# Sorted experts of a routed MLP: tokens stationary and gate and up moved together as 256 columns, the loop written out, deeper rings, 47 tiles

## The chip, the core and the metric

The program runs on one core of a Trainium2 chip. The metric is the device time of one execution in microseconds (us); a lower number is better. Nothing runs on the other cores.

## The reference, cut to what matters

The program computes two layers over 2048 tokens of width 512: a state-space layer with a routed MLP behind it, then attention with a quantised MLP behind it, each followed by a layer norm. The change lies in the routed MLP alone:

```python
gate = zeros((T, E)).at[arange(T)[:, None], idx].add(vals)      # the best 2 of 16 experts per token
def step(y, p):
    w1, b1, w2, b2, w3, b3, ge = p
    h = silu(xt @ w1 + b1) * (xt @ w2 + b2)                     # 512 -> 128, twice
    return y + ge[:, None] * (h @ w3 + b3), None                # 128 -> 512
y, _ = scan(step, zeros_like(xt), (ew1, eb1, ew2, eb2, ew3, eb3, gate.T))
```

## The kernel before, in words

`program` calls the stages one after the other, each in a block of its own that all engines leave together: `ssm`, `normalise` (ln1), `route_and_share`, `sorted_experts`, `normalise` (ln2, which gathers the experts' rows), `project`, `attend`, `attention_out`, `normalise` (ln3), `quantised_mlp`. In `route_and_share` each token's row is scattered twice into `sorted_x` in HBM, sorted by expert and padded so that every run of 128 rows (a tile, `P`) belongs to one expert; `g.owner` holds the expert of each tile. `SORTED` (L30) is the number of tiles, 47 rounded up to a multiple of `TURN`, so 48.

`sorted_experts` (L1199) works through these tiles. Per tile j it loads 256 KB of rows and 769 KB of weights and biases of the owner (gate and up: the first `WUP` = 1024 columns; down: the next 512), computes, and stores 256 KB. Every product is made in three matmuls of float32r parts (`three`, L126): stationary and moving operand are each split into a high part (a rounded copy) and a low part (the rest), and high·high, high·low and low·high are summed in PSUM.

The steps of tile j, with the function that issues each:

- SP: `load_x`, `load_w`, `store_y`. `load_w` waits until the buffer of tile j-4 is free (`up_lo`, `down_lo`, `h_ready`), reads the owner into a register and issues the DMA. Four weight buffers and four row buffers. In SP's order `store_y` comes 4 tiles late, behind the two loads of the same step.
- PE: `turn` (four 128x128 transposes of the rows), `up` (gate and then up, 4 chunks by 3 matmuls each: the weights are stationary, the turned tokens move as 128 columns, 24 matmuls in all; gate and up come out with the hidden unit in the partition), `down` (3 matmuls of 512 columns, the hidden activations stationary).
- ACT: `x_hi` (L1344), `down_weights_hi` (L1350), `gate` (silu, L1356), `h_hi` (L1363), `y_copy` (L1338).
- DVE: `x_lo` (L1376), `up_weights_lo` (L1381), `hidden` (L1387), `h_lo` (L1392).
- POOL: `up_weights_hi` (L1281), `down_weights_lo` (L1287).

`steps` sets the order on each engine: a list of (lag, function) pairs, so that step n does tile n - lag of each. The first `TURN` steps and the last are written out; those between run in a hardware loop (`Fori`) with four tiles in the body and semaphore values computed from the loop's register. Before: SP (0, load_x) (0, load_w) (4, store_y); PE (0, turn) (1, up) (2, down); ACT (3, y_copy) (0, x_hi) (1, down_weights_hi) (1, gate) (1, h_hi); DVE (0, x_lo) (0, up_weights_lo) (1, hidden) (1, h_lo); POOL (0, up_weights_hi) (1, down_weights_lo). The split weights `g.wh`, `g.wl` have two buffers, and so have the turned tokens, the hidden parts, `y` and each PSUM tile. `SORTED` also sets how many zero tiles `ssm` stores into `sorted_x` and the width of the small owner computation in `route_and_share`.

Of the kernel before, what the change touches and what calls it, by code (L numbers as in the profile page):

```python
# [8 lines left out]
F32 = mybir.dt.float32  # L9
# [5 lines left out]
P = 128  # L15
# [13 lines left out]
TURN = 4  # L29
SORTED = -(-(TOP * TILES + EXPERTS - 1) // TURN) * TURN  # L30
# [640 lines left out]
def normalise(nc, g, tag, by_feature, out=None, quantise=False, gather=False, ahead=None):  # L671
# [5 lines left out]
    with ExitStack() as ctx:  # L677
# [215 lines left out]
def route_and_share(nc, a, g):  # L893


    with ExitStack() as ctx:
# [49 lines left out]
        turned, gate_ready, dve_chain, scattered = sem("turned"), sem("gate_ready"), sem("dve_chain"), sem("scattered")  # L946
# [252 lines left out]
def sorted_experts(nc, a, g):  # L1199
# [4 lines left out]
    with ExitStack() as ctx:  # L1204
        sb, ps, sem = scoped(nc, ctx, "exp", reused=True)
        raw = g.raw + [sb(f"raw{k}", [P, WN + 2]) for k in range(2, TURN)]
        x = [sb(f"x{k}", [P, DIM]) for k in range(TURN)]
# [4 lines left out]
        y = [sb(f"y{k}", [P, DIM]) for k in range(2)]  # L1212
        pt = [ps(f"pt{k}", [P, KC, P]) for k in range(2)]

        pgu = [[ps(f"p{n}{k}", [P, NB]) for n in "gu"] for k in range(2)]
        py = [ps(f"py{k}", [P, DIM]) for k in range(2)]
        x_in, w_in = [sem(f"x_in{k}") for k in range(TURN)], [sem(f"w_in{k}") for k in range(TURN)]
        up_hi, down_hi, xh_ready, g_ready = sem("up_hi"), sem("down_hi"), sem("xh_ready"), sem("g_ready")
        s_ready, hh_ready, hl_ready = sem("s_ready"), sem("hh_ready"), sem("hl_ready")


        y_stored = [sem(f"y_stored{k}") for k in range(2)]
        x_turned, xl_ready, u_ready, h_ready = sem("x_turned"), sem("xl_ready"), sem("u_ready"), sem("h_ready")
        up_lo, down_lo, y_ready, y_copied = sem("up_lo"), sem("down_lo"), sem("y_ready"), sem("y_copied")
        AHEAD = TURN
        block = ctx.enter_context(nc.Block())

        def steps(eng, stages):

            for n in range(TURN):  # L1230
                for lag, do in stages:
                    if n >= lag:
                        do(n - lag, n - lag)
            with eng.Fori(1, SORTED // TURN) as i:
                for n in range(TURN):
                    for lag, do in stages:
                        do(i * TURN + (n - lag), (n - lag) % TURN)
            for n in range(max(lag for lag, _ in stages)):
                for lag, do in stages:
                    if n < lag:  # L1240
                        do(SORTED + n - lag, (n - lag) % TURN)

        @block.sync
        def _(sp):
            def load_x(j, s):

                sp.wait_ge(x_turned, j - TURN + 1 + AHEAD)
                sp.dma_start(x[s][:].unsqueeze(1), g.sorted_x.rearrange("(t p) d -> p t d", p=P)[:, bass.ds(j, 1), :]
                             ).then_inc(x_in[s], 16)

            def load_w(j, s):

                sp.wait_ge(up_lo, j - TURN + 1 + AHEAD)
                sp.wait_ge(down_lo, j - TURN + 1 + AHEAD)
                sp.wait_ge(h_ready, j - TURN + 1 + AHEAD)
                e = nc.values_load(g.owner[0:1, bass.ds(j, 1)], engines=(mybir.EngineType.SP,), min_val=0,
                                   max_val=EXPERTS - 1)
                sp.dma_start(raw[s][:].unsqueeze(1), a["w123"][bass.ds(e, 1)].rearrange("e p w -> p e w")
                             ).then_inc(w_in[s], 16)

            def store_y(j, s):
                sp.wait_ge(y_copied, j + 1 + AHEAD)
                sp.dma_start(g.sorted_y.rearrange("(t p) d -> p t d", p=P)[:, bass.ds(j, 1), :], y[s % 2][:].unsqueeze(1)
                             ).then_inc(y_stored[s % 2], 16)

            for k in range(2):
                sp.sem_inc(y_stored[k], 16)
            steps(sp, [(0, load_x), (0, load_w), (TURN, store_y)])
            for k in range(2):
                sp.wait_ge(y_stored[k], 16 * SORTED // 2 + 16)  # L1270

        @block.gpsimd
        def _(pool):
            pool.sem_inc(down_lo, AHEAD)

            def up_weights_hi(j, s):

                pool.wait_ge(w_in[s], (j - s) * (16 // TURN) + 16)

                wait_apart(pool, u_ready, j - 1 + AHEAD)  # L1280
                nc.gpsimd.tensor_scalar(g.wh[s % 2][:, 0:WUP], raw[s][:, 0:WUP], 1.0, 0.0, ALU.mult,  # L1281
                                        ALU.add).then_inc(up_hi, 1)

            def down_weights_lo(j, s):
                pool.wait_ge(down_hi, j + 1)
                wait_apart(pool, y_ready, j - 1 + AHEAD)
                nc.gpsimd.tensor_tensor(g.wl[s % 2][:, WUP:WN], raw[s][:, WUP:WN], g.wh[s % 2][:, WUP:WN].bitcast(F32),  # L1287
                                        ALU.subtract).then_inc(down_lo, 1)
# [983 lines left out]
```

## Time and profile before

| | us |
|---|---|
| runs | 2175.79, 2177.35, 2159.76 |
| median | 2175.79 |
| profiled execution | 2182.81 (span 2181.1) |
| mean granted TensorE clock | 0.908 of full |
| busy: PE / DVE / ACT / POOL | 83% / 72% / 38% / 36% of the span |

The stage of this change runs from its first DMA issue at 659.7 to the next stage's first instructions at 901.8 us of the span. A line of a timeline gives start, duration, engine, line of the kernel, operation and tiles (out<-in); matmuls overlap, so the distance between two starts is what one costs. The 1.2 and 2.4 GHz levels of TensorE's clock are shown as 0.50 and 1.00.

### The profile page before, as it was taken

The page shows a single profiled execution, that of the slowest core. Times are in us where ns is not written, and L with a number is a line of the kernel's source. Part 1 is how long each engine was busy: PE and PEld are TensorE (multiplying, and loading weights), DVE is VectorE, ACT ScalarE, POOL GpSimd, SP SyncE. Part 2 cuts the span into 40 slices and gives each one's busy share as a digit, 9 for nine tenths or more (in the row PEclk, how much of TensorE's full clock was granted, in tenths as well). Part 3 has the DMA queues.
Part 4 walks back from the last instruction along what each step waited for, and adds up shares of the span by engine and source line. Part 5 has one row for each costly group of instructions (what it writes and reads, how often), then busy time and mean ns, then how long its engine had stood idle before and what let it go on. Part 6 is the DMA issues. An engine that isn't in the chain of part 4 may idle for free. (4 is left out here: it accounts for less than half of the span.)

```text
span 2181.1 us, 26434 instructions
## 1 busy us (share of the span) xinstructions
PE 1810.3 (83%) x8264; PEld 1133.3 (52%) x8264; DVE 1567.4 (72%) x2851; ACT 832.6 (38%) x1362; POOL 779.1 (36%) x469
## 2 busy tenths in 40 slices
PE   5888878776598999539958888888936999999998
PEld 1232323224367888428833333333724877777786
DVE  6999999996435765582138888887388677667668
ACT  4646464432113544312217777777232111111112
POOL 4898989862504766551011000000033133212200
PEclk7999989998787987759969999999966999999999
DMA  4333334220306887535553333331001000000002
GB/s 126 103 116 97 116 107 115 83 62 19 137 17 225 300 287 257 187 120 194 193 158 96 88 97 85 93 92 46 1 31 44 15 30 30 30 1 30 1 1 78
DMA packets 111213, 212.99 MB, mean 98 GB/s; under 512 B 18953, under 2 KB 35721, under 8 KB 110203
## 3 DMA queue, kind: packets, MB, share of 16 engines
q1 hardware_dynamic: 105979, 194.80, 28.6%
q0 software_dynamic: 5120, 16.78, 2.4%
q8 instruction: 58, 0.95, 0.2%
q14 instruction: 56, 0.46, 0.1%
HBM read 145.92 MB, written 63.18 MB: 96 GB/s over the span
## 5 line engine op out<-in xcount | busy, mean ns | idle before, releaser
L1773 DVE TENSOR_REDUCE att_top<-att_first 128x1 f32<-128x512 f32 x512 | 332.3, 686 | 101.9 <-PE att_first L1653 94.3
L552 DVE TENSOR_TENSOR_SCAN ssm_h<-ssm_da,ssm_dbx 128x512 f32<-128x512 f32 x256 | 305.5, 1212 | 6.4 <-ACT ssm_da L422 6.1
L292 POOL TENSOR_TENSOR ssm_dbx<-ssm_u,ssm_bbc 128x2048 f32<-128x2048 f32 x63 | 285.0, 4524 | 47.9 <-DVE ssm_h L552 46.4
L635 PE MATMUL ssm_y<-ssm_hc,all_ident 128*128 128x512 f32 x396 | 228.7, 667 | 73.9 <-DVE ssm_hc L503 68.9
L1735 ACT ACTIVATE att_prob<-att_second 128x1024 f32<-128x1024 f32 x256 | 248.0, 1022 | 86.6 <-PE att_second L1673 81.2
L422 ACT ACTIVATE ssm_da<-ssm_dt,ssm_minus_a 128x512 f32<-128x512 f32 x256 | 176.7, 690 | 200.8 <-DVE ssm_h L552 200.5
L1919 POOL TENSOR_TENSOR pairs_raw<-pairs_raw,pairs_scales 128x512 f32<-128x512 f32 x42 | 42.2, 1040 | 532.1 <-DMA pairs_raw<-in_w 532.1
L2049 ACT ACTIVATE ffn_silu<-ffn_pg 128x256 f32<-128x256 f32 x112 | 43.1, 385 | 415.4 <-PE ffn_pg L130 415.3
L1653 PE MATMUL att_first<-att_ks,att_qs 48*128 48x512 f32 x512 | 133.6, 510 | 63.2 <-DVE att_top L1773 48.4
L128 PE MATMUL ffn_pg<-pairs_wh,last_XH 128*128 128x512 f32 x448 | 180.1, 402 | 1.7 <-PEq L677 1.7
L129 PE MATMUL ffn_pg<-pairs_wl,last_XH 128*128 128x512 f32 x448 | 178.8, 399 | 0.0
L130 PE MATMUL ffn_pg<-pairs_wh,last_XL 128*128 128x512 f32 x448 | 178.1, 397 | 0.0
L635 PEld LDWEIGHTS ssm_y<-ssm_hc,all_ident 128*128 128x128 f32 x396 | 65.8, 201 | 186.7 <-DVE ssm_hc L503 131.6
L1653 PEld LDWEIGHTS att_first<-att_ks,att_qs 48*128 48x128 f32 x512 | 53.5, 190 | 192.2 <-DVE att_top L1773 131.4
L2073 DVE TENSOR_TENSOR ffn_h<-ffn_pg,ffn_silu 128x256 f32<-128x256 f32 x112 | 47.4, 423 | 134.6 <-ACT ffn_silu L2049 134.5
L503 DVE TENSOR_TENSOR ssm_hc<-ssm_cbc,ssm_h 128x512 f32<-128x512 f32 x198 | 132.5, 669 | 14.2 <-issue 7.1
L1688 PE MATMUL att_out<-att_prob,att_v 128*32 128x512 f32 x1024 | 137.2, 608 | 0.1
L1926 POOL TENSOR_SCALAR pairs_wh<-pairs_raw 128x512 fp32r<-128x512 f32 x42 | 24.9, 625 | 238.7 <-PE ffn_py L130 238.7
L128 PE MATMUL ffn_py<-pairs_wh,ffn_hh 128*128 128x512 f32 x224 | 97.8, 437 | 0.2 <-DVE ffn_hl L2091 0.2
L130 PEld LDWEIGHTS ffn_pg<-pairs_wh,last_XL 128*128 128x128 f32 x448 | 85.5, 191 | 21.7
L128 PEld LDWEIGHTS ffn_pg<-pairs_wh,last_XH 128*128 128x128 f32 x448 | 85.0, 190 | 22.4 <-issue 2.0
L129 PEld LDWEIGHTS ffn_pg<-pairs_wl,last_XH 128*128 128x128 f32 x448 | 85.0, 190 | 20.7
(294 smaller groups left out, 4095.5 us busy)
## 6 DMA issues: line engine op xcount, KB each, us to landing
mlps_raw<-in_w SPq DMA_DIRECT2D x26, 769.0 KB, 5.8
exp_raw<-in_w SPq DMA_DIRECT2D x24, 769.0 KB, 5.8
ssm_bbc<-brow_dram SPq DMA_DIRECT2D x64, 256.0 KB, 4.1
ssm_cbs<-crow_dram SPq DMA_DIRECT2D x58, 256.0 KB, 3.5
sorted_x<-ssm_zero SPq DMA_DIRECT2D x48, 256.0 KB, 3.7
exp_x<-sorted_x SPq DMA_DIRECT2D x48, 256.0 KB, 3.8
sorted_y<-exp_y SPq DMA_DIRECT2D x48, 256.0 KB, 3.3
att_qs<-qk_dram SPq DMA_DIRECT2D x192, 64.0 KB, 2.2
```

Of the source, the lines that this page charges most:

```text
L128: pe.matmul(out, lh, rh, start=first, stop=False)
L129: pe.matmul(out, lh, rl, start=False, stop=False)
L130: return pe.matmul(out, ll, rh, start=False, stop=last)
L292: nc.gpsimd.tensor_tensor(dbx[:, n % 2], u[:, n // STATE % 2], bbc[:, n % RING, :].unsqueeze(1).to_broadcast([P, KC, NB]), ALU.mult).then_ ...
L422: nc.scalar.activation(da[:, i % 2, :], dt[:, b % 2, c, :], ACT.Exp, scale=minus_a[:, c, n % STATE:n % STATE + 1]).then_inc(da_ready, 1)
L503: nc.vector.tensor_tensor(hc[:, k % 2, :], cbc[:], h[:, n % 2, c, :], ALU.mult).then_inc(hc_ready, 1)
L552: nc.vector.tensor_tensor_scan(h[:, n % 2, c, :], da[:, i % 2, :], dbx[:, n % 2, c, :], 0.0, ALU.mult, ALU.add).then_inc(h_ready, 1)
L635: pe.matmul(y[:, c, :], g.ident[:], hc[:, k % 2, :], start=(m == 0), stop=(m == STATE - 1)).then_inc(y_own, 1)
L1653: pe.matmul(p_first[first_place(m) % FIRSTS][:], qs[w % RING][at, pair, qt * P:(qt + 1) * P], ks[w % RING][at, pair, :], start=True, stop= ...
L1688: mm = pe.matmul(p_out[VPAD * j:VPAD * (j + 1), :], v[s % RING][:, kt, VPAD * j:VPAD * (j + 1)], prob[step % 2][:, j, :], start=(kt == 0), ...
L1735: nc.scalar.activation(prob[step % 2][:, js, :], p_second[second_place(step, pair) % 2][:], ACT.Exp, scale=DK ** -0.5).then_inc(exp_done, 1)
L1773: nc.vector.tensor_reduce(top[w % 2][:, qt, item:item + 1], p_first[first_place(m) % FIRSTS][:], AX.X, ALU.max).then_inc(max_done, 1)
```

## The change

The gate and up product is turned round: the turned tokens are stationary, and the gate and up weights of one 128-row chunk move together as 256 columns, so `up` has 12 matmuls of 256 columns. The result has the token in the partition; it is copied from PSUM to SBUF by ACT (`copy_gu`), turned back by two transposes on PE (`turn_gu`), and read from PSUM by `gate` and `hidden`. The hardware loop is replaced by steps that are all written out, with constant semaphore values. Weight buffers: 7, five of them inside `g.X`; row buffers 6; y buffers 4; split down weights 4, two of them inside `g.XL`. The store is issued 8 steps late. 47 tiles. Some DMA semaphores are made once for the whole program.

```diff
-TURN = 4
-SORTED = -(-(TOP * TILES + EXPERTS - 1) // TURN) * TURN
+SORTED = TOP * TILES + EXPERTS - 1
...
-            gathered = [sem(f"gathered{k}") for k in range(GRING)]
+            gathered = g.gathered
...
+        RAWS, XS, DOWNS, YS = 7, 6, 4, 4
+        GU = 2 * INTER
...
+        raw = ([r[:] for r in g.raw] + [inside(g.X[:], k) for k in range(5)])
+        x = [sb(f"x{k}", [P, DIM]) for k in range(XS)]
+        gu = [sb(f"gu{k}", [P, GU]) for k in range(2)]
+        y = [sb(f"y{k}", [P, DIM]) for k in range(YS)]
+        spare = g.XL[:].rearrange("p c t -> p (c t)")
+        down_h = [g.wh[k][:, WUP:WN] for k in range(2)] + [spare[:, k * DIM:(k + 1) * DIM] for k in range(2)]
+        down_l = [g.wl[k][:, WUP:WN] for k in range(2)] + [spare[:, k * DIM:(k + 1) * DIM] for k in range(2, 4)]
+        pgu = [ps(f"pgu{k}", [P, NB]) for k in range(2)]
+        pr = [ps(f"pr{k}", [P, NB]) for k in range(2)]
...
+        def steps(stages):
+            for n in range(SORTED + max(lag for lag, _ in stages)):
+                for lag, do in stages:
+                    if 0 <= n - lag < SORTED:
+                        do(n - lag)
...
+            def load_w(j):
+                if j >= RAWS:
+                    sp.wait_ge(up_lo, j - RAWS + 1)
+                    sp.wait_ge(down_lo, j - RAWS + 1)
+                    sp.wait_ge(h_ready, j - RAWS + 1)
...
-            steps(sp, [(0, load_x), (0, load_w), (TURN, store_y)])
+            steps([(0, load_x), (0, load_w), (RAWS + 1, store_y)])
...
+            def up_weights_hi(j):
+                arrived(pool, w_in, j)
+                if j >= 2:
+                    pool.wait_ge(gu_ready, j - 1)
...
             def down_weights_lo(j):
                 pool.wait_ge(down_hi, j + 1)
-                wait_apart(pool, y_ready, j - 1 + AHEAD)
...
-                for n, ready in ((0, g_ready), (1, u_ready)):
-                    for c in range(KC):
-                        w = slice((n * KC + c) * INTER, (n * KC + c + 1) * INTER)
-                        mm = three(pe, pgu[k][n][:, 0:P], g.wh[k][:, w], g.wl[k][:, w], xh[k][:, c, :], xl[k][:, c, :],
-                                   c == 0, c == KC - 1)
-                    mm.then_inc(ready, 1)
+                if j >= 2:
+                    pe.wait_ge(gu_copied, j - 1)
+                both = [w[k][:, 0:WUP].rearrange("p (n c i) -> p c n i", n=2, c=KC) for w in (g.wh, g.wl)]
+                out = pgu[k][:, 0:GU].rearrange("p (n i) -> p n i", n=2)
+                for c in range(KC):
+                    mm = three(pe, out, xh[k][:, c, :], xl[k][:, c, :], both[0][:, c], both[1][:, c], c == 0, c == KC - 1)
+                mm.then_inc(gu_ready, 1)
+
+            def turn_gu(j):
+                pe.wait_ge(gu_copied, j + 1)
+                if j >= 2:
+                    pe.wait_ge(h_ready, j - 1)
+                for n in range(2):
+                    mm = pe.transpose(pr[j % 2][:, n * P:(n + 1) * P], gu[j % 2][:, n * P:(n + 1) * P], g.ident[:])
+                mm.then_inc(gu_turned, 1)
...
-            steps(pe, [(0, turn), (1, up), (2, down)])
+            steps([(0, turn), (2, turn_gu), (1, up), (3, down)])
...
+            def copy_gu(j):
+                act.wait_ge(gu_ready, j + 1)
+                if j >= 2:
+                    act.wait_ge(gu_turned, j - 1)
+                nc.scalar.activation(gu[j % 2][:], pgu[j % 2][:, 0:GU], ACT.Copy).then_inc(gu_copied, 1)
+
+            def y_copy(j):
+                act.wait_ge(y_ready, j + 1)
+                if j >= YS:
+                    act.wait_ge(y_stored[j % YS], 16 * (j // YS))
+                nc.scalar.activation(y[j % YS][:], py[j % 2][:], ACT.Copy).then_inc(y_copied, 1)
...
-            steps(act, [(3, y_copy), (0, x_hi), (1, down_weights_hi), (1, gate), (1, h_hi)])
+            steps([(0, x_hi), (2, gate), (0, down_weights_hi), (2, h_hi), (1, copy_gu), (3, y_copy)])
...
-            steps(dve, [(0, x_lo), (0, up_weights_lo), (1, hidden), (1, h_lo)])
+            steps([(0, x_lo), (2, hidden), (0, up_weights_lo), (2, h_lo)])
...
+        g.scattered, g.gathered = sem("scattered"), [sem(f"gathered{k}") for k in range(4)]
```

POOL's list is as before, (0, up_weights_hi) (1, down_weights_lo).

## Rows read from the trace of the kernel before

**Rows 1.** Windows: busy us and instruction count of each engine, granted clock, DMA share, GB/s.
```profile
659.70:901.80 242.10, 217.10 (x1488) 202.90 (x1488) 145.87 (x192) 106.90 (x240) 147.03 (x96) 0.86 0.78 260
721.00:775.00 54.00, 48.13 (x381) 44.70 (x381) 39.47 (x50) 25.87 (x61) 37.30 (x25) 1.00 0.91 312
857.80:877.80 20.00, 20.00 (x87) 18.81 (x87) 8.90 (x13) 7.17 (x16) 10.01 (x6) 0.50 0.63 207
664.00:673.00 9.00, 5.55 (x25) 5.18 (x26) 4.61 (x4) 1.48 (x3) 3.33 (x3) 0.50 0.98 378
773.00:776.00 3.00, 1.41 (x12) 1.24 (x10) 2.62 (x3) 0.95 (x3) 1.38 (x2) 0.95 0.89 321
722.00:725.00 3.00, 1.68 (x16) 1.56 (x15) 1.88 (x3) 1.25 (x3) 1.25 (x2) 1.00 0.92 336
```

**Rows 2.** Weight tiles, whole stage: POOL's rounding; duration min/median/max, first and last start.
```profile
L1281 POOL TENSOR_SCALAR mlps_wh<-mlps_raw x24: 1038/1046/1122, 666.2 to 880.2; 128x1024 fp32r<-128x1024 f32 x24
L1281 POOL TENSOR_SCALAR mlps_wh<-exp_raw x24: 1039/1047/1097, 674.1 to 889.3; 128x1024 fp32r<-128x1024 f32 x24
```

**Rows 3.** Timeline of PE at full clock, 783.8 to 785.4.
```profile
783.76 0.27 PE L130 MATMUL exp_pu<-exp_xh,mlps_wl 128*128 128x128 f32 x1
...
784.43 0.28 PE L130 MATMUL exp_pu<-exp_xh,mlps_wl 128*128 128x128 f32 x1
...
785.07 0.40 PE L130 MATMUL exp_py<-mlps_wh,exp_hl 128*128 128x512 f32 x1
785.31 0.60 PE L1303 MATMUL exp_pt<-all_ident,exp_x 128*128 128x128 f32 x4
```

**Rows 4.** Timeline of PE at half clock, 781.4 to 781.7.
```profile
781.47 0.41 PE L129 MATMUL exp_pg<-exp_xl,mlps_wh 128*128 128x128 f32 x1
781.68 0.41 PE L130 MATMUL exp_pg<-exp_xh,mlps_wl 128*128 128x128 f32 x1
```

**Rows 5.** DMA, 721 to 775: queue share, then issues, KB each, median us to landing.
```profile
q1 hardware_dynamic: 5570, 16.84, 91.3%
...
mlps_raw<-in_w SPq DMA_DIRECT2D x7, 769.0 KB, 5.9
exp_raw<-in_w SPq DMA_DIRECT2D x6, 769.0 KB, 5.6
```

**Rows 6.** Waits, 721 to 775, and SP's own wait, 700 to 880: total us, times, longest.
```profile
POOL mlps_wh L1281 <- DMA mlps_raw<-in_w: 5.3, 4, 2.0
...
SPq L1263 <- ACT exp_y L1338: 79.2, 38, 4.8
```

**Rows 7.** Groups of ACT by form, 721 to 775: busy us, mean ns | idle before.
```profile
L1344 ACT ACTIVATE exp_xh<-exp_pt 128x512 fp32r<-128x512 f32 x12 | 7.1, 591 | 0.0
L1338 ACT ACTIVATE exp_y<-exp_py 128x512 f32<-128x512 f32 x12 | 7.0, 587 | 0.9 <-issue 0.5 <-PE exp_py L130 0.4
L1363 ACT ACTIVATE exp_hh<-exp_h 128x128 fp32r<-128x128 f32 x13 | 4.0, 311 | 28.2 <-DVE exp_h L1387 28.2
L1350 ACT ACTIVATE mlps_wh<-exp_raw 128x512 fp32r<-128x512 f32 x6 | 3.8, 632 | 0.0
L1356 ACT ACTIVATE exp_silu<-exp_pg,exp_raw 128x128 f32<-128x128 f32 x6 | 2.2, 368 | 0.0
```

**Rows 8.** From the page's costliest groups: an ACT read of 256 PSUM columns, in another stage.
```profile
L2049 ACT ACTIVATE ffn_silu<-ffn_pg 128x256 f32<-128x256 f32 x112 | 43.1, 385 | 415.4 <-PE ffn_pg L130 415.3
```

**Rows 9.** Groups of DVE by form, 721 to 775.
```profile
L1376 DVE TENSOR_TENSOR exp_xl<-exp_pt,exp_xh 128x512 fp32r<-128x512 f32 x12 | 8.3, 692 | 6.0 <-ACT exp_xh L1344 6.0
L1392 DVE TENSOR_TENSOR exp_hl<-exp_h,exp_hh 128x128 fp32r<-128x128 f32 x12 | 7.2, 596 | 4.5 <-ACT exp_hh L1363 4.5
L1387 DVE SCALAR_TENSOR_TENSOR exp_h<-exp_pu,exp_raw,exp_silu 128x128 f32<-128x128 f32 x7 | 2.4, 344 | 0.0
```

**Rows 10.** Splitting of weights, whole stage: duration ns min/median/max.
```profile
L1381 DVE TENSOR_TENSOR mlps_wl<-exp_raw,mlps_wh x24: 1215/1216/2315, 676.1 to 890.4; 128x1024 fp32r<-128x1024 f32 x24
L1287 POOL TENSOR_TENSOR mlps_wl<-exp_raw,mlps_wh x24: 1267/2254/2346, 683.4 to 894.5; 128x512 fp32r<-128x512 f32 x24
```

More of the change, by code:

```diff
@@ L1218, in sorted_experts @@
[L1218 to L1225, printed above, removed]
+        x_in, w_in = [sem(f"x_in{k}") for k in range(XS)], [sem(f"w_in{k}") for k in range(RAWS)]
@@ L1226, in sorted_experts, with arrived @@
         block = ctx.enter_context(nc.Block())
-        def steps(eng, stages):
-            for n in range(TURN):
+        def arrived(eng, sems, j):
+            eng.wait_ge(sems[j % len(sems)], 16 * (j // len(sems) + 1))
+        def steps(stages):
+            for n in range(SORTED + max(lag for lag, _ in stages)):
                 for lag, do in stages:
[L1232 to L1241, printed above, removed]
+                    if 0 <= n - lag < SORTED:
+                        do(n - lag)
@@ L1243, in _ @@
         @block.sync
         def _(sp):
[L1245 to L1259, printed above, removed]
@@ L1359, in h_hi, with x_hi @@
-            def h_hi(j, s):
-                act.wait_ge(h_ready, j + 1 + AHEAD)
-                act.wait_ge(y_ready, j - 1 + AHEAD)
-                nc.scalar.activation(hh[s % 2][:], h[s % 2][:], ACT.Copy).then_inc(hh_ready, 1)
-            steps(act, [(3, y_copy), (0, x_hi), (1, down_weights_hi), (1, gate), (1, h_hi)])
+            def x_hi(j):
+                act.wait_ge(x_turned, j + 1)
+                if j >= 2:
+                    act.wait_ge(gu_ready, j - 1)
+                nc.scalar.activation(xh[j % 2][:], pt[j % 2][:], ACT.Copy).then_inc(xh_ready, 1)
@@ new lines, in gate, with down_weights_hi @@
+            def gate(j):
+                act.wait_ge(gu_turned, j + 1)
+                if j >= 2:
+                    act.wait_ge(h_ready, j - 1)
+                nc.scalar.activation(silu[j % 2][:], pr[j % 2][:, 0:INTER], ACT.Silu,
+                                     bias=raw[j % RAWS][:, WN:WN + 1]).then_inc(s_ready, 1)
+            def down_weights_hi(j):
+                arrived(act, w_in, j)
+                if j >= DOWNS:
+                    act.wait_ge(y_ready, j - DOWNS + 1)
+                nc.scalar.activation(down_h[j % DOWNS], raw[j % RAWS][:, WUP:WN], ACT.Copy).then_inc(down_hi, 1)
@@ new lines, in h_hi @@
+            def h_hi(j):
+                act.wait_ge(h_ready, j + 1)
+                if j >= 2:
+                    act.wait_ge(y_ready, j - 1)
+                nc.scalar.activation(hh[j % 2][:], h[j % 2][:], ACT.Copy).then_inc(hh_ready, 1)
+            def copy_gu(j):
+                act.wait_ge(gu_ready, j + 1)
+                if j >= 2:
+                    act.wait_ge(gu_turned, j - 1)
+                nc.scalar.activation(gu[j % 2][:], pgu[j % 2][:, 0:GU], ACT.Copy).then_inc(gu_copied, 1)
@@ L1373, in x_lo, with hidden @@
-            def x_lo(j, s):
+            def x_lo(j):
                 dve.wait_ge(xh_ready, j + 1)
-                nc.vector.tensor_tensor(xl[s % 2][:], pt[s % 2][:], xh[s % 2][:].bitcast(F32),
+                nc.vector.tensor_tensor(xl[j % 2][:], pt[j % 2][:], xh[j % 2][:].bitcast(F32),
                                         ALU.subtract).then_inc(xl_ready, 1)
-            def up_weights_lo(j, s):
+            def hidden(j):
+                dve.wait_ge(s_ready, j + 1)
+                if j >= 2:
+                    dve.wait_ge(hl_ready, j - 1)
+                nc.vector.scalar_tensor_tensor(out=h[j % 2][:], in0=pr[j % 2][:, INTER:GU], scalar=raw[j % RAWS][:, WN + 1:WN + 2],
+                                               in1=silu[j % 2][:], op0=ALU.add, op1=ALU.mult).then_inc(h_ready, 1)
```

113 lines of the change are left out of this document (44 added, 69 removed).

## Prediction

> **What bounds the kernel now.** I read the windows over the stage first, then PE's timeline, the DMA queues, the waits, and the groups of ACT, DVE and POOL. In the windows [rows 1] the stage of the sorted experts takes 242.1 us of the 2181 us span; PE is busy for 90% of it, at a mean clock of 0.86, and the DMA share is 0.78. That mean hides two regimes. From 721 to 775 the clock is full and the DMA queues are at 0.91 and 312 GB/s; from 857.8 to 877.8 the clock is half, PE never stops, and DMA falls to 0.63. The pace follows from POOL's first instruction on each tile, which starts at 666.2 for tile 0 and at 889.3 for tile 47 [rows 2]: 223.1 / 47 = 4.75 us per tile.
>
> At full clock PE starts a 128-column matmul every 0.67 / 6 = 0.112 us and a 512-column one every 0.24 us [rows 3]. A tile has 4 transposes, 24 matmuls of 128 and 3 of 512: 28 x 0.112 + 3 x 0.24 = 3.86 us. At half clock a 128-column matmul comes every 0.21 us [rows 4], so I double that to about 7.3 us. Even at full clock the pace isn't PE's: 13 weight loads went out in the 54 us [rows 5], so 4.15 to 4.35 us per tile. The waits say why [rows 6]: POOL waits for weights (up to 2.0 us), and SP sat 79 us of 180 in front of `store_y`, for ACT's copy of y of four tiles ago, with the next two loads behind it. So the four buffers don't give four tiles of lead. Every third tile or so the weights are late, PE runs dry, and after some of these gaps the clock falls: in 773 to 776 PE was busy for 1.41 of 3 us and the clock began to fall at the end; in 722 to 725 it was busy for 1.68 and the clock stayed full [rows 1]. Three things bound the stage, each at about 4 us per tile: PE, the loads, and the half clock that their collisions bring.
>
> **The parts of the change.**
>
> *PE.* 24 matmuls of 128 columns become 12 of 256, with 2 transposes more. No row has 256 columns in float32r. Bounds: not under the 0.112 of a 128-column one; by a straight line between 128 and 512 columns 0.112 + 0.128 / 3 = 0.155; at worst twice a 128-column one, 0.224. Half of the 512-column spacing is 0.12. I take 0.13, nearest to that row, because the moving operand is the larger part from there on. A tile then costs 6 x 0.112 + 12 x 0.13 + 3 x 0.24 = 2.95 us at full clock (2.7 to 4.1), about 5.6 at half. PE stops being a bound at full clock.
>
> *ACT.* Before: 0.591 + 0.587 + 0.311 + 0.632 + 0.368 = 2.49 us per tile [rows 7]. `copy_gu` adds a read of 256 PSUM columns; another stage has one at 0.385 [rows 8], with 0.37 (128 columns) and 0.59 (512) as ends. Sum 2.88 us. Behind `x_hi` on ACT, `x_lo` (0.69) and `hidden` (0.34) of DVE [rows 9] stand before `h_hi`, while `gate` and `down_weights_hi` take 1.0 of that. One round of ACT is then copy 0.385, y 0.59, x_hi 0.59, DVE 1.04, h_hi 0.31 and some six handovers of up to 0.1: 2.9 to 3.5 us. The new waits: `turn_gu` waits for `copy_gu`, and PE has `down` of another tile (0.72) and `turn` (0.45) in between, so it costs nothing; if that cover went, 0.385 a tile would be on PE's path and PE would still be at 3.3.
>
> *DVE and POOL.* The same instructions in the same number. But they get in each other's way: `down_weights_lo` takes 1.27 or 2.25 to 2.35 us, `up_weights_lo` 1.22 or 2.3 [rows 10], and one of each pair always has the longer value. The pair costs 2.3 us together, `up_weights_hi` 1.05 [rows 2] and `h_lo` 0.3 to 0.6 [rows 9] stand beside it: 3.65 to 3.95 us per tile. That is a floor that the change doesn't touch.
>
> The Trainium skill, SBUF — State Buffer, section Who interferes with whom, says that a GpSimd instruction and a DVE one with two SBUF inputs hold one port pair exclusively; the trace agrees, with 1.22 + 1.1 = 2.3.
>
> *DMA.* Per tile 769 + 256 + 256 = 1281 KB = 1.312 MB, unchanged. At 312 GB/s that is 4.2 us; the same queues at a share of 1.0 instead of 0.91 would do 343 GB/s, 3.83 us; loads alone ran at 378 GB/s in 664 to 673 [rows 1], 3.47 us. With seven weight buffers and the store 8 steps late SP no longer waits for a fresh y before the next load, so the queues stay filled. I take a share of 0.945, 324 GB/s: **4.05 us per tile**, nearest to the measured 0.91, since even with more queued the completions and collisions remain. `y_copy` j waits for store j-4, which SP issues behind the loads of tile j+4. ACT then stands there until those loads are through, with `x_hi`, `gate` and `copy_gu` behind it. SP needs only `h_ready` of tile j-3 for these loads, which ACT made two steps earlier, so the loads are already queued: the wait paces ACT at the DMA's rate and adds nothing to it.
>
> The Trainium skill, DMA: Bandwidth & Descriptors, section Where 436 GB/s comes from, has about 358 GB/s as the limit between HBM and a core. The start of the stage, at 378, is above it. By that figure a tile would take 3.66 us and the sum below would come out at about -55 us.
>
> *The loop, 47 tiles, the rest.* One tile less is counted below. The loop's branch, the register arithmetic and the separate nops go; they're inside the 4.75. One zero store of 48 goes in `ssm`, where they are awaited only at the stage's end, hundreds of us later: nothing, and under a microsecond of SP's issue if that cover were gone. The owner rows shrink by 1/48. Semaphores moved to the whole program: nothing. Head: SP issues load_x 0 and load_w 0 first, as before, so 0. Tail (889.3 to 901.8): a copy of 0.385 and two transposes more, an `up` of 12 x 0.13 in place of 24 x 0.112: about -0.5 to 0; the eight late stores are 2.1 MB, 6.5 us at 324 GB/s, beside that tail. Together 0, up to +3.
>
> **Sum.** Before: 47 intervals, 223.1 us. After: 46 x 4.05 = 186.3 us. Difference -36.8 us, in the profiled execution's terms 2182.8 - 36.8 = 2146. That execution lies 7 us above the median of the runs; the same difference from the median gives 2175.8 - 36.8 = **2139 us**. From 3.9 to 4.3 us per tile: -44 to -25, 2132 to 2151.
>
> **Rivals.**
>
> 1. *The queues in order bind, not the DMA* (17%). ACT's round of 3.5, and the DVE and POOL port of up to 3.95, are close enough to 4.05 to lengthen each other; at full clock the pace was 4.3 with PE at 3.86, so part of that may be theirs. Against it: in those 54 us POOL's waits name the weights. 4.3 to 4.65 us: -25 to -9 us, 2151 to 2167.
>
> 2. *Slower: the half clock settles in* (7%). With loads at 4.05 and PE at 2.95, PE rests over 1 us in every tile instead of 1.5 in every third. If these rests bring the clock down each time, PE needs about 5.6 us per tile. Over all 46 that is 258 us, +34, 2210. It decides once the mean pace passes 223.1 / 46 = 4.85 us, that is once some 60% of the tiles run at half clock. Against it: the shorter of the two gaps above, 1.32 us of rest, didn't lower the clock, the rests are spread, and while PE runs at half clock it doesn't rest, the buffers fill, and the next tiles run back to back.
>
>  The Trainium skill, TensorE: Matmul & The Clock Gate, section Loop structure matters more than you think, warns of just this: a DMA wait between bursts of matmuls lets PE go cold. By that rule this rival would be the likeliest and the time about 2210; the rows of the two gaps show it for the longer one alone.
>
> 3. *256 columns cost what two times 128 cost* (6%). Then PE is at 6 x 0.112 + 12 x 0.224 + 0.72 = 4.08, the stage stays as it is in kind, and only the deeper rings help: 4.4 to 4.75, -21 to -5, about 2164. The 512-column spacing of 0.24, far from 4 x 0.112, speaks against it.
>
> 4. *The mix runs as fast as loads alone* (8%). Then the port and ACT bind at 3.65: 46 x 3.65 = 168, -55, 2121.
>
> **Numbers.** Forecast 62%. A measurement of this kernel tells about 1%, 22 us, from no change: faster means below 2154, slower above 2197. Faster: 0.60 of the forecast, 0.08 of rival 4, 0.06 of rival 1: 0.74. Same: the rest of rivals 1 and 3 and some of the forecast and of rival 2: 0.20. Slower: 0.06. The range takes the forecast with an offset of a few us between sets of runs, rival 4 at its edge and most of rival 1: 2120 to 2164.
>
> **What the profile after would show.** Right: POOL's first instructions of tile 0 and 46 about 186 us apart; DMA share 0.93 or more at 320 GB/s and over through the middle; matmuls of 256 columns 0.12 to 0.15 us apart; PE busy for three quarters of the stage with short rests at full clock; landings of weights well over 6 us, since they queue; SP waiting in `load_w` and not in `store_y`. Wrong: a DMA share under 0.88 with DVE or ACT without rests (rival 1), a granted clock under 0.8 over the stage (rival 2), 0.2 us between matmuls of 256 columns (rival 3). A pace under 3.8 would mean that the DMA's cost was read too high.

## The result, and the profile after

| | before | after |
|---|---|---|
| runs, us | 2175.79, 2177.35, 2159.76, 2180.29 | 2091.79, 2089.09, 2090.92, 2090.25 |
| median, us | 2176.57 | 2090.59 |
| ratio, 95% interval | | 0.9619 [0.9569, 0.9669] |
| profiled execution, us | 2182.81 (span 2181.1) | 2091.79 (span 2090.1) |
| mean granted clock | 0.908 | 0.923 |

After is 86 us faster; forecast were 37, and the time lies below the range. The two profiled spans differ by 91.0 us: 74.7 in the sorted experts (242.1 against 167.4), 16.4 in the stage ahead of them, `route_and_share` (135.4 against 119.0), 2 in `ssm`, and 2 given back behind the experts. The 16.4 turn out not to be the change's (experiments e5, e9, e13 to e15). Compared on one chip, in two launches where every profile has the short routing stage, the change gives 73.5 and 77.8 us (e5, e13).

The windows of the experts' stage and of its middle, in the columns of [rows 1]:

```profile
641.60:809.00 167.40, 144.47 (x987) 124.23 (x987) 152.19 (x188) 113.83 (x282) 150.33 (x94) 0.97 0.93 370
680.00:780.00 100.00, 92.69 (x652) 80.61 (x651) 100.00 (x125) 74.49 (x187) 99.98 (x63) 1.00 1.03 411
```

DVE and POOL have no rest, the DMA queues are at a share of 1.03 and 411 GB/s without a dip, PE is busy for 93% at the full clock. POOL's rounding, which gave the pace in [rows 2]:

```profile
L1280 POOL TENSOR_SCALAR mlps_wh<-all_X x33: 1724/2022/2035, 653.5 to 795.2; 128x1024 fp32r<-128x1024 f32 x33
L1280 POOL TENSOR_SCALAR mlps_wh<-mlps_raw x14: 1047/2021/2035, 647.7 to 785.4; 128x1024 fp32r<-128x1024 f32 x14
```

From tile 0 to tile 46 are 795.2 - 647.7 = 147.5 us, 3.21 us per tile, against 223.1 us and 4.75. That difference, 75.6, is the stage's. The same instruction of 1.05 us in [rows 2] now takes 2.02: it waits inside its own span, as the timelines of POOL and DVE show (start, duration, instruction):

```profile
700.35 1.32 POOL L1285 TENSOR_TENSOR later_XL<-mlps_raw,later_XL 128x512 fp32r<-128x512 f32 x1
701.63 2.03 POOL L1280 TENSOR_SCALAR mlps_wh<-all_X 128x1024 fp32r<-128x1024 f32 x1
703.63 1.32 POOL L1285 TENSOR_TENSOR mlps_wl<-all_X,mlps_wh 128x512 fp32r<-128x512 f32 x1
```
```profile
700.44 0.68 DVE L1385 TENSOR_TENSOR exp_xl<-exp_pt,exp_xh 128x512 fp32r<-128x512 f32 x1
701.04 0.34 DVE L1393 SCALAR_TENSOR_TENSOR exp_h<-exp_pr,mlps_raw,exp_silu 128x128 f32<-128x128 f32 x1
701.30 1.45 DVE L1398 TENSOR_TENSOR mlps_wl<-all_X,mlps_wh 128x1024 fp32r<-128x1024 f32 x1
702.67 1.12 DVE L1403 TENSOR_TENSOR exp_hl<-exp_h,exp_hh 128x128 fp32r<-128x128 f32 x1
```

`h_lo`, 128 columns, takes 1.12 us, as long as it needs until POOL's 1024 columns are through. So engines at 100% are not yet proof of the bound; e6 to e8 ask that.

PE's timeline: the new matmuls start 0.12 us apart, and PE rests 0.28 us in this tile (7.3 of 100 us over the middle, 0.23 per tile).

```profile
700.71 0.28 PE L127 MATMUL exp_pgu<-mlps_wh,exp_xh 128*128 128x256 f32 x1
700.83 0.28 PE L128 MATMUL exp_pgu<-mlps_wl,exp_xh 128*128 128x256 f32 x1
700.95 0.28 PE L129 MATMUL exp_pgu<-mlps_wh,exp_xl 128*128 128x256 f32 x1
...
702.85 0.35 PE L127 MATMUL exp_pgu<-mlps_wh,exp_xh 128*128 128x256 f32 x1 [0.28 <-issue]
```

SP's own wait, 660 to 785 (total us, times, longest), is in `load_w` alone; in [rows 6] it was in `store_y`. Loads now take 9.1 us from issue to landing (680 to 780), against 5.6 to 5.9 in [rows 5], because they stand in a full queue:

```profile
SPq L1253 <- DVE exp_h L1393: 34.9, 37, 1.2
```
```profile
q1 hardware_dynamic: 13507, 40.94, 102.6%
...
all_X<-in_w SPq DMA_DIRECT2D x22, 769.0 KB, 9.1
sorted_y<-exp_y SPq DMA_DIRECT2D x32, 256.0 KB, 9.4
```

### The profile page after: what moved, and what is told of

Read it like the earlier page. It is cut to its first block and busy times, and to the rows that moved or that the text cites. A ratio compares the mean times of both kernels' runs of the same rounds, so it can differ in the third digit from the quotient of the medians.

```text
span 2090.1 us, 24698 instructions
## 1 busy us (share of the span) xinstructions
PE 1727.8 (83%) x7763; PEld 1052.6 (50%) x7763; DVE 1571.3 (75%) x2847; ACT 839.0 (40%) x1404; POOL 783.8 (38%) x467
## 3 DMA queue, kind: packets, MB, share of 16 engines
q8 instruction: 64, 1.05, 0.2%
```

## The experiments

Four theories for the 4.75 us per tile of before: Q, the loads come late because of the rings and of the store's place on SP; P, PE's orientation; O or L, the old order of the steps, or the loop; and for what holds after at 3.2, S, the port of DVE and POOL, against D, the DMA's bytes. The table has the time, the median of before on the same chip, the ratio with its interval, the pace (first to last start of POOL's rounding), and the length of the routing stage, which shows whether the 16 us are there: at 134 to 136 the total holds them, at 118 or 119 it doesn't. Totals of the two kinds can't be set against each other, so the readings below go by the pace. The intervals of e1, e9, e14 and e17 hold 1; e17's total alone shows no gain. Each pace is that of one profiled execution.

| | us | before | ratio | us per tile | routing |
|---|---|---|---|---|---|
| e1 loop written out | 2178.14 | 2179.18 | 0.9976 [0.9940, 1.0011] | 4.63 | 134 |
| e2 rings only | 2145.23 | 2179.18 | 0.9818 [0.9779, 0.9857] | 4.00 | 136 |
| e3 after, old orientation | 2145.57 | 2179.18 | 0.9825 [0.9785, 0.9866] | 3.93 | 135 |
| e4 after, four buffers | 2138.10 | 2179.18 | 0.9791 [0.9752, 0.9830] | 3.94 | 135 |
| e5 after | 2090.45 | 2163.99 | 0.9650 [0.9615, 0.9685] | 3.20 | 119 |
| e6 half of the up low part | 2089.62 | 2163.99 | 0.9655 [0.9612, 0.9697] | 3.12 | 119 |
| e7 half of the rows loaded | 2086.72 | 2163.99 | 0.9641 [0.9599, 0.9684] | 3.20 | 119 |
| e8 both halves | 2073.88 | 2163.99 | 0.9582 [0.9537, 0.9627] | 2.87 | 118 |
| e9 before | 2181.61 | 2180.42 | 1.0017 [0.9997, 1.0037] | 4.72 | 135 |
| e10 as e4 | 2139.98 | 2180.42 | 0.9802 [0.9728, 0.9877] | 3.93 | 135 |
| e11 seven weights, store 5 back | 2133.18 | 2180.42 | 0.9771 [0.9697, 0.9846] | 3.74 | 135 |
| e12 four weights, store 8 back | 2167.53 | 2180.42 | 0.9914 [0.9884, 0.9944] | 4.57 | 135 |
| e13 after | 2086.77 | 2164.53 | 0.9644 [0.9605, 0.9684] | 3.21 | 118 |
| e14 before | 2169.64 | 2164.53 | 1.0008 [0.9966, 1.0049] | 4.68 | 119 |
| e15 as e3 | 2127.25 | 2164.53 | 0.9832 [0.9758, 0.9906] | 3.94 | 118 |
| e16 e11, store by ACT | 2088.95 | 2164.53 | 0.9655 [0.9614, 0.9695] | 3.23 | 119 |
| e17 before, store by ACT | 2158.86 | 2192.24 | 0.9875 [0.9737, 1.0013] | 4.24 | 135 |
| e18 e4, store by ACT | 2148.57 | 2192.24 | 0.9828 [0.9692, 0.9963] | 4.11 | 135 |

**e1: the loop alone.**

```diff
-            with eng.Fori(1, SORTED // TURN) as i:
+            for i in range(1, SORTED // TURN):
```

> The kernel before with its loop of eleven passes written out; buffers, order of the steps, orientation and 48 tiles as they were. Theory Q (the rings are what was short: four buffers and a store queued four tiles back leave the DMA queue near empty, and deep rings keep it at 411 GB/s, 3.19 us for a tile's bytes): the experts stage stays near 242 us, 4.6 to 4.75 us a tile, time within 10 us of before. Theory L (what ended was the loop's cost: addresses from registers and the jump at every fourth tile): the stage falls to 170 to 205 us, time 35 to 70 us under before. Theory P (the matmuls' orientation): as Q here. Beside it, the 16 us by which the routing stage became shorter: if that comes from the semaphores made once, the routing stage stays near 135 us here; if from the program as a whole, it may be 119.

4.63 against 4.68 to 4.75 in three profiles of the kernel before: the loop was worth at most a tenth of a microsecond per tile, 5 us, which the total doesn't resolve. Routing stayed at 134 us with the program unrolled. SP still waits at the store, 41.1 of 100 us (before: 43.8 in the same window, 680 to 780):

```profile
SPq L1263 <- ACT exp_y L1338: 41.1, 23, 3.8
```

**e2: the rings alone** (e1's written-out loop; orientation, order, 48 tiles as before; seven weight buffers, six for rows, four for y, and the semaphores that are made once).

```diff
-        raw = g.raw + [sb(f"raw{k}", [P, WN + 2]) for k in range(2, TURN)]
+        RAWS, XS, YS = 7, 6, 4
...
+        raw = ([r[:] for r in g.raw] + [inside(g.X[:], k) for k in range(5)])
...
-            steps(sp, [(0, load_x), (0, load_w), (TURN, store_y)])
+            steps(sp, [(0, load_x), (0, load_w), (RAWS + 1, store_y)])
```

> The kernel before, loop written out, with the seven weight buffers, six x, four y, the store eight tiles back and the semaphores of routing made once; order of the steps on PE, ACT, DVE, POOL and the orientation (24 matmuls of 128 columns) as before, 48 tiles. Theory Q: the queue is no longer the limit and the rest runs at what PE needs at full clock, 3.86 us, or at the lags of the old order: 3.9 to 4.3 us a tile, experts stage 190 to 210 us, time 30 to 50 us under before. Theory P (PE's orientation alone set the pace, in the chain through PE at half clock): 4.6 us a tile and 235 to 245 us of stage. Theory O (the old order, in which each engine waits for the next, sets the pace): 4.3 to 4.7 us a tile, 210 to 230 us.

4.00 us per tile, and 3.82 between tiles 8 and 39, where PE never stops: what the prediction worked out for PE alone (3.86). Theory Q holds as far as that; the rings bring 0.63 us over e1. O is out: the old order runs at PE's own pace. The window 680 to 780:

```profile
680.00:780.00 100.00, 100.00 (x769) 95.09 (x769) 63.80 (x100) 57.09 (x125) 80.83 (x50) 0.94 0.93 329
```

**e3: after with the old orientation.**

```diff
+                for n, out in ((0, pgu[k]), (1, pr[k])):
+                    for c in range(KC):
+                        w = slice((n * KC + c) * INTER, (n * KC + c + 1) * INTER)
+                        mm = three(pe, out[:, 0:P], g.wh[k][:, w], g.wl[k][:, w], xh[k][:, c, :], xl[k][:, c, :], ...)
...
-            steps([(0, turn), (2, turn_gu), (1, up), (3, down)])
+            steps([(0, turn), (1, up), (3, down)])
```

> The kernel after with the old orientation: 24 matmuls of 128 columns with the weights held, gate in one bank and up in the other, no copy of the results by ACT and no turning back; rings, order with its lags, down copies, 47 tiles and the loop written out as in after. Theory P (orientation): PE needs 3.86 us a tile instead of 2.9, so 3.9 to 4.2 us a tile, stage 185 to 200 us, time 2110 to 2125 us; if PE also falls back to the half clock, 4.5 us and 2140 or more. Theory Q alone (rings are all): 3.2 to 3.4 us a tile, time within 8 us of after. Twelve of 256 save nothing only if 24 of 128 at spacing 0.118/2 keep up, and then this kernel is as fast as after or faster, with ACT's 0.37 us copy gone.

PE binds at 3.82 in the middle again, so beside PE's bound after's order changes nothing in the pace; whether it would under a lower bound isn't shown. The new orientation on these rings is worth 3.93 - 3.21 = 0.72 us. The total missed its expected 2110 to 2125: 2145.57 here with the 16 us of routing, 2127.25 in e15 without them. Read the DMA share of this one (720 to 780):

```profile
720.00:780.00 60.00, 60.00 (x491) 57.28 (x490) 36.25 (x63) 34.43 (x80) 35.87 (x32) 1.00 0.99 344
```

PE is the bound here, the queues only wait for work, and yet their share is 0.99 at 344 GB/s. After carries 411 at 1.03. **The share isn't a use of the capacity**: a packet of 6152 bytes (a row of the weights) has its median at 235 to 238 ns in all of these kernels, but its mean is 239 ns in after, 298 in e3 and 311 in before (680 to 780), with a tail beyond 1 us where fewer transfers are queued. Only the slowest fifth or so of the packets differs (the 80th percentile is 239, 245 and 270 ns), and it fills the share.

**e4 and e10: after with four buffers.**

```diff
-        RAWS, XS, DOWNS, YS = 7, 6, 4, 4
+        RAWS, XS, DOWNS, YS = 4, 4, 4, 4
```

With RAWS the store moves to five tiles back.

> The kernel after with four weight buffers and four x, and the store five tiles back in place of eight. Theory Q: with four in the ring the loads are asked for late again; landings of 9 us against 3 tiles of lead leave 3.6 to 4.2 us a tile, stage 185 to 215 us, time 20 to 45 us over after. Theories P and O (orientation or order): 3.2 us a tile holds, since a load needs about 5 us by itself, and the time is within 5 us of after.

> The kernel after with four weight buffers, four x and the store five tiles back, a second time. If the crawl belongs to the chip, it is here only if before has it too on this chip; time 2122 without it, 2138 with it. If to the program: crawl and 2138 us. Pace of the experts stage 3.94 us a tile as the first time.

3.94 and 3.93: without the rings 0.69 of the 1.42 us are there (4.63 to 3.94), without the orientation 0.6 to 0.7 (e2, e3). Neither alone does it. The 0.69 aren't the orientation's alone, though: against e1, e4 also has four y buffers, the new order and the store one step later, and SP's wait at the store falls from 41.1 to 11.8 of 100 us. With the store off SP in both, the pair e17 and e18 leaves 0.13 us for orientation and order together (4.24 to 4.11; between tiles 8 and 39 it is even 4.04 to 4.21), so with four buffers what the orientation alone is worth isn't shown. The window 680 to 780 of e4 bears on the clock too: PE rests 22 of 100 us, 0.9 us per tile on average and up to 1.7 at once, at a granted clock of 0.98.

```profile
680.00:780.00 100.00, 78.17 (x532) 66.32 (x530) 83.39 (x101) 64.64 (x151) 56.87 (x51) 0.98 0.94 334
```

**e5: after again**, on another chip.

> The kernel after, unchanged, a second time, to see whether the 16 us in the routing stage are its own. In the stage of routing PE issues one instruction each 0.70 us for 16 us in the profiled run of before and of the first four experiments, and at full pace in that of after. If the difference comes with the program, the time is 2089 to 2092 us again and the crawl is absent; if it comes with the chip or the execution, the crawl is there, the routing stage lasts 135 us and the time is near 2106 us.

2090.45 us at 3.20 us per tile, without the crawl. By this expectation that spoke for the program; the launches below show that it isn't so.

**e6, e7, e8: what holds after at 3.2?** e6 leaves out half of the low part of the gate and up weights, e7 half of each row of tokens, e8 both; none computes the whole result.

```diff
-                nc.vector.tensor_tensor(g.wl[j % 2][:, 0:WUP], raw[j % RAWS][:, 0:WUP], g.wh[j % 2][:, 0:WUP].bitcast(F32),
+                width = WUP if j < 2 else WUP // 2
+                nc.vector.tensor_tensor(g.wl[j % 2][:, 0:width], raw[j % RAWS][:, 0:width], g.wh[j % 2][:, 0:width].bitcast(F32),
```
```diff
-                sp.dma_start(x[j % XS][:], g.sorted_x.rearrange("(t p) d -> p t d", p=P)[:, j, :]).then_inc(x_in[j % XS], 16)
+                width = DIM if j < XS else DIM // 2
+                sp.dma_start(x[j % XS][:, 0:width], g.sorted_x.rearrange("(t p) d -> p t d", p=P)[:, j, 0:width]).then_inc(x_in[j % XS], 16)
```

> The kernel after, with DVE computing the low part of the up and gate weights on 512 of the 1024 columns from tile 2 on (the rest of the low part is stale and the output is off): 0.6 us less of DVE's work that excludes POOL's. What sets after's 3.2 us a tile? Theory S (DVE and POOL, taking turns at their shared port): 2.6 to 2.9 us a tile if the loads can follow, that is, 12 to 25 us less; DMA's theory D (bytes at 411 GB/s): 3.2 us a tile, no change within 3 us; both at once (S and D bind at the same value): 3.2 here and 3.2 in the next one, and under 3.0 only with both.

> The kernel after, with load_x fetching 256 of 512 columns of the sorted rows from tile 6 on (the other half is stale and the output is off): 131 KB less of 1.31 MB a tile. Theory D: 2.88 us a tile, 13 us less. Theory S: 3.2 us a tile, the DMA share falls to 0.9 and the time stays within 3 us of after.

> Both reductions together. If DMA and the shared port bind at the same value, this alone falls clearly under 3.1 us a tile, to 2.9 (PE's own 2.9 us a tile is the next floor, and ACT's near 2.9): 13 us less than after. If one of the two had bound alone, the same time as that experiment.

The windows 680 to 780, one fence for each kernel, in this order:

```profile
680.00:780.00 100.00, 92.82 (x657) 79.97 (x657) 79.92 (x125) 76.15 (x187) 72.55 (x64) 1.00 1.03 411
```
```profile
680.00:780.00 100.00, 92.69 (x654) 80.69 (x654) 100.00 (x125) 74.17 (x187) 100.00 (x63) 1.00 1.01 368
```
```profile
680.00:780.00 100.00, 99.73 (x744) 90.52 (x743) 91.37 (x142) 86.23 (x212) 92.82 (x71) 1.00 1.03 407
```

With the port relieved DVE falls to 80% and POOL to 73%, and the pace stays (3.19 in the middle, e6): the DMA holds it at 411 GB/s. With the DMA relieved it falls to 368 GB/s and the pace stays at 3.23: DVE and POOL hold it at 100%. With both relieved it goes to 2.81 in the middle and 2.87 from first to last tile. So the two bind at the same 3.2 us. Next in line are two again: PE at 99.7%, and the DMA, for which the 1.18 MB of e8's tile at 411 GB/s are 2.87 us; e8 runs at 407. The total falls by 16.6 us against e5, more than the expected 13.

POOL's rounding takes 1.16 us on average in e6, 2.0 in after and e7, which is the wait inside the instruction again. The Trainium skill, SBUF — State Buffer, section Who interferes with whom, says that a DVE instruction with two inputs in SBUF contends with a GpSimd instruction that reads SBUF. The trace agrees: it's the `TENSOR_TENSOR` of 128 columns that takes 1.12 us beside POOL's read.

**e11 and e12: which ring?**

```diff
-        RAWS, XS, DOWNS, YS = 7, 6, 4, 4
+        RAWS, XS, DOWNS, YS = 7, 4, 4, 4
-            steps([(0, load_x), (0, load_w), (RAWS + 1, store_y)])
+            steps([(0, load_x), (0, load_w), (5, store_y)])
```

e12 has RAWS 4, XS 6, YS 4 and the store 8 steps back.

> The kernel after with four x and the store five tiles back, the seven weight buffers kept: which of the two rings gives the 0.74 us a tile between four buffers (3.94) and after (3.20)? If the weight ring: 3.2 us a tile, time within 5 us of after (2090). If the store, which waits on SP ahead of the next loads, or the x ring: 3.6 to 3.9 us a tile, 20 to 35 us over after.

> The other half: four weight buffers, six x and the store eight tiles back. If the weight ring is what counts: 3.8 to 4.0 us a tile, time 25 to 35 us over after. If the store or the x ring: 3.2 to 3.4 us a tile.

e11 keeps all seven weight buffers and is back at 3.74, so three more buffers bring 0.2 us over e4 and e10 as long as the store stays five back. The waits of SP (680 to 780) are at the store, and POOL waits for weights.

```profile
SPq L1266 <- ACT exp_y L1377: 32.5, 26, 2.6
SPq L1254 <- DVE mlps_wl L1398: 1.0, 4, 0.3
SPq L1262 <- PE exp_pt L1298: 0.4, 1, 0.4
```

e12 was expected at 3.8 to 4.0 and fell to 4.57, nearly to the kernel before. It is the other side of the same queue: SP waits 53.3 us in `load_w`, the store stands behind it, and ACT waits for that store with four y buffers. This is the cover of which the prediction spoke ("the loads are already queued"), with the cover gone:

```profile
DVE exp_xl L1385 <- ACT exp_xh L1341: 40.4, 18, 3.9
ACT exp_y L1377 <- DMA sorted_y<-exp_y: 35.9, 18, 3.5
```

**e16: e11 with the store on ACT's queue.**

```diff
-            steps([(0, load_x), (0, load_w), (5, store_y)])
+            steps([(0, load_x), (0, load_w)])
...
+            def store_y(j):
+                act.wait_ge(y_copied, j + 1)
+                act.dma_start(g.sorted_y.rearrange("(t p) d -> p t d", p=P)[:, j, :], y[j % YS][:]
+                              ).then_inc(y_stored[j % YS], 16)
```

> The kernel of e11 (seven weight buffers, four x) with the store of y issued by ACT one tile after its copy, and SP left with the loads alone. If it was the store's wait on SP, ahead of the next loads, that held e11 at 3.79 us a tile: 3.2 to 3.3 here, 24 to 28 us less than e11. If it was the x ring of four: 3.7 to 3.8 and no gain.

3.23 us per tile and 408 GB/s, with only four x buffers: in e11 it was the store's wait on SP. All of SP's waiting is now for its x buffers, and it costs nothing, since the queue is full:

```profile
SPq L1262 <- PE exp_pt L1293: 43.1, 31, 1.8
```
```profile
680.00:780.00 100.00, 92.47 (x653) 80.41 (x651) 100.00 (x125) 74.26 (x188) 100.00 (x64) 1.00 1.03 408
```

**e17 and e18: the store off SP with four weight buffers.** The same edit in e1's kernel (with four y) and in e4's.

> The kernel before with its loop written out (worth 0.1 us a tile by e1), the store of y issued by ACT at the end of the step in which it makes the copy, and four y; SP has only the loads; four weight buffers, four x, old orientation, 48 tiles. If the store's wait on SP made the loads late: PE's own 3.82 to 4.0 us a tile, stage 190 to 200 us, 30 to 40 us less than before on the same chip. If four weight buffers are too few even so: 4.3 to 4.6 us, within 15 us of before.

> The variant of after with four weight buffers and four x, its store issued by ACT as in e16. If the number of weight buffers doesn't matter once the store is off SP: 3.2 us a tile like e16. If four leave too little lead for landings of about 9 us at a full queue: 3.4 to 3.8 us a tile, 10 to 28 us over e16 in like state of the routing stage.

Both missed their paces. e17 gains 0.4 us per tile on e1 (4.24; 4.04 in the middle), more than half of what the rings gave, but doesn't reach PE's 3.82. (ACT never waited for a store in e1's 680 to 780, so the two more y buffers don't explain it.) Its total is 33 us under before, inside the expected 30 to 40, with an interval that holds 1. e18 isn't faster than e4 but slower, 4.11 against 3.94. It differs from e16 in the number of weight buffers alone: seven in place of four are worth 4.11 - 3.23 = 0.88 us once the store is off SP, against 0.2 with it there. The windows of e17 and e18:

```profile
680.00:780.00 100.00, 97.43 (x769) 92.14 (x767) 70.56 (x98) 54.93 (x124) 77.50 (x49) 0.97 0.92 316
```
```profile
680.00:780.00 100.00, 76.62 (x522) 65.32 (x521) 79.44 (x99) 62.84 (x150) 54.87 (x50) 0.98 0.95 323
```

In both SP now waits in `load_w`; e18:

```profile
SPq L1253 <- DVE exp_h L1393: 58.7, 25, 3.6
SPq L1262 <- PE exp_pt L1293: 1.0, 2, 0.7
```

This fits the ring's round trip. In e18 `hidden` of a tile ends 8.9 us (median) after POOL's rounding of it starts, and only then is its buffer free; a load takes 6.7 to 7.0 us to land. 8.9 + 6.9 = 15.8 us, plus the handovers, have to fit into four tiles: 4 x 4.11 = 16.4. With seven buffers, after has 7 x 3.21 = 22.5 us for 9.4 + 9.1 = 18.5. The 8.9 us are themselves two steps of the order and grow with the pace, so this is a consistency and no price. Why e18 is slower than e4 is open; both trips are longer there (8.5 and 6.0 to 6.6 in e4).

**e9, e13, e14, e15: whose are the 16 us in routing?** In the profile of before and in e1 to e4, PE goes into a crawl at about 590 us: for some 16 us its matmuls start 0.70 us or a multiple of it apart (591.27, 591.98, 594.77 and 596.16 in e9), with no wait shown, until about the end of the indirect scatters at 605. After hadn't it. These are the kernels before, after and e3's, unchanged.

> The kernel before, unchanged, on the chip of the next three, with a profile. After and its three variants ran on one chip without the crawl of PE in routing (one instruction each 0.70 us for 16 us), experiments one to four on another chip with it; so chip and kernel can't be told apart yet. If the crawl belongs to the chip, all four kernels of this call have it or none. If it belongs to the program, this one has it (routing 135 us, time near 2175) whatever the others show.

> The kernel after, unchanged, on the chip of the next three. If the crawl of PE in routing belongs to the kernel: absent here, present in e14 and e15, times 2090, 2178 and 2145. If it belongs to the chip: present or absent in all alike, and the times move together by 16 us (2106, 2178, 2145 with it; 2090, 2162, 2129 without).

> The kernel before, unchanged. As above: with the crawl 2178 us and routing 135 us, without it 2162 us and 119 us.

> The kernel after with the old orientation (weights held, 24 matmuls of 128 columns), a second time. The experts stage at 3.82 us a tile as the first time. Crawl by kernel: 2145 us; by chip and absent: 2129 us.

The kernel before, with the crawl (e9) and without it (e14), same columns as above:

```profile
590.00:606.00 16.00, 5.38 (x11) 2.40 (x11) 1.46 (x3) 0.63 (x1) 9.23 (x10) 0.62 0.45 172
```
```profile
590.00:606.00 16.00, 16.00 (x63) 11.49 (x62) 4.30 (x7) 2.01 (x3) 9.31 (x10) 1.00 0.45 170
```

PE issues 11 matmuls in one and 63 in the other, from the same program. In all eight profiled runs of two launches (e5 to e8, e13 to e16) the crawl is absent, in all ten of three others (e1 to e4, e9 to e12, e17, e18) present, whatever the kernel. Where it is absent the kernel before runs in 2164 us, in the other three launches in 2179 to 2192. So it doesn't go with the change. Each launch was on a chip of its own, so chip and launch can't be told apart. In the comparison at the top three of the four runs of before lie at 2176 to 2180, and its profile has the crawl; on which chips they ran isn't recorded. Its mechanism stays open.

## Why the prediction was right in sign and missed by half

**The sign and the mechanism hold**, and so does most of the list of what the profile would show: landings well over 6 us, SP waiting in `load_w`, full clock through the middle, matmuls of 256 columns 0.12 apart. Not met were the 186 us between POOL's first instructions of tile 0 and 46 (147.5) and PE busy for three quarters of the stage (86%). The change's own gain, by e5 and e13 without the crawl, is 2163.99 - 2090.45 = 73.5 us and 2164.53 - 2086.77 = 77.8, with ratios of 0.9650 [0.9615, 0.9685] and 0.9644 [0.9605, 0.9684]. Against that stand 36.8 forecast.

**The step that failed is the DMA term**: "the same queues at a share of 1.0 instead of 0.91 would do 343 GB/s, 3.83 us ... I take a share of 0.945, 324 GB/s: 4.05 us per tile." Measured: 411 GB/s, 3.19 us for the same 1.312 MB. 46 x (4.05 - 3.21) = 39 us, the whole miss of the stage. With the DMA right the prediction would still have stopped at its next floor, the 3.65 of DVE and POOL: 18 of the 39 us are the DMA term's, 20 the floor's, below. The mistake is to scale a rate by a busy share; e3 has a share of 0.99 at 344 GB/s where the DMA isn't the bound at all. The loads alone of [rows 1], 378 GB/s over 9 us, were nearer, and single microseconds in it already ran at 418 to 441. The prediction's own last sentence names this case: "a pace under 3.8 would mean that the DMA's cost was read too high."

The prediction read the four-tile store and its wait of 79 us from [rows 6], and then let the DMA's rate and not that wait set the price. e11, e16 and e17 show what it was worth: 0.5 us per tile with seven buffers (e11 to e16), 0.4 in the kernel before with its loop written out (e1 to e17).

**The floor of DVE and POOL** was put at 3.65 to 3.95 and is 3.2 (e7). It was a sum in series of the pair (2.3), `up_weights_hi` (1.05) and `h_lo` (0.3 to 0.6). But 0.6 for `h_lo` already held a wait (it takes 0.28 us throughout e3, and 0.29 at the least in before), and the instructions of the two engines overlap in part: in the timelines above POOL's `down_weights_lo` runs until 701.67 beside three instructions of DVE, the last of them `up_weights_lo` from 701.30. Which overlap is worth how much isn't shown. This floor also closed the range from below, through rival 4 ("the port and ACT bind at 3.65"). That rival, at 8%, was the nearest to what came; nothing was left for a pace under 3.65.

**PE.** 2.95 us were put, with 0.13 for 256 columns. Measured: 0.118, so 6 x 0.112 + 12 x 0.118 + 0.72 = 2.81, and e8 ran at that in its middle. For the old orientation 3.86 were put; e2 and e3 ran at 3.82. Both right.

**ACT.** 2.88 us of work were put; the groups of after give 0.598 + 0.592 + 0.312 + 0.644 + 0.373 + 0.367 = 2.89. `copy_gu` had 0.385 and measured:

```profile
L1370 ACT ACTIVATE exp_gu<-exp_pgu 128x256 f32<-128x256 f32 x39 | 14.3, 367 | 0.0
```

**The wait of `y_copy` at nothing**: right for after, where the middle shows none; e12 shows the price when the loads ahead of the store have to wait, 36 of 100 us. **The loop inside the 4.75**: e1, at most 0.1 us per tile. **Head and tail at 0 to 3**: the head was 6.5 us (659.7 to 666.2) and is 6.1, the tail was 12.5 (889.3 to 901.8) and is 13.8 (795.2 to 809.0): +1.

**The rivals.** Rival 1, that the order binds: e2 runs the old order at PE's pace, so no; but in after the port does bind, at 3.2 beside the DMA. Rival 2, the half clock: PE rested 0.23 us per tile in after and the granted clock was 1.00; in e4 it rested 0.9 us per tile at 0.98. The rule about loop structure by which the Trainium skill (TensorE: Matmul & The Clock Gate, Loop structure matters more than you think) made this rival the likeliest, a long DMA wait between bursts, doesn't decide in these two. In e12 PE is busy for as much as in e4 (78.3 of 100 us, 680 to 780), and the mean clock is 0.90: the way to rival 2 exists. PE's rests there are no longer than in e4, 1.5 us at most against 1.7, so what brings the clock down in one and not in the other stays open. Rival 3 is out by the spacing of 0.118.

**The baseline.** Of the 86 us, 8 to 13 aren't the change's, by the 73.5 and 77.8 above; of the 91.0 between the two profiles the 16.4 in routing are the crawl. This forecast couldn't have had it.

The Trainium skill, DMA: Bandwidth & Descriptors, section Where 436 GB/s comes from, has about 358 GB/s as what binds between HBM and a core. The trace disagrees: 411 GB/s over 100 us, reads and writes together, with nothing running on the other cores. It stays below the 435 that the section gives for the side of SBUF.

No version here that does the whole work beats after beyond the uncertainty: e16 (2088.95) and e13 (2086.77) on one chip have ratios whose intervals overlap. To go under 3.2 both bounds would have to give at once, and PE's 2.81 is 18 us away.

## What to carry to other kernels

Don't scale a DMA rate by the busy share: look at the median packet against the mean, and at the rate in the best slices; here the mean lay well above the median (298 and 311 ns against 235) where the queue was short of work, and on it (239 against 238) where the DMA held the pace (e6) or helped to hold it (after). Before pricing a load as bandwidth, list what stands ahead of it on its issuing queue: a store that waits for a fresh result holds back all loads behind it, and deeper load buffers bring little until it is moved back or to another queue (0.2 us, e4 to e11, against 0.88, e18 to e16); moving the store without the buffers brought nothing (e4 to e18). And when a bound is removed, price the next two: here PE stood at 3.8 us per tile and the kernels with four buffers at 3.9, and each alone gave about half.

## What was not expected of the hardware

- PE's crawl: matmuls at multiples of 0.70 us for some 16 us, in three launches on three chips and not in two on others, at the same place of the same program, and no wait recorded. A single profile made it look like a gain of the change.
- A DMA share above 1: 1.03 at 411 GB/s, and 1.01 at 368 in e7, so the last tenth of that scale says little of the rate.
- Waits of DVE and POOL for each other stand inside the durations (1.05 or 2.02 us, 0.3 or 1.12 us), so both engines show 100% busy where one of them could do with 73% (e6).
